# The first batch of a four-batch transformer layer reordered: queries and keys ahead of values, weight splits moved, the Hadamard fold of a weight rebuilt, one wait shortened

## The reference

```
x = x + layernorm(attention(layernorm(x)))      16 heads of 16, causal, rope on q and k
x = x + layernorm(ffn(layernorm(x)))
attention: qkv = x @ w_qkv.T + b_qkv; softmax(q k^T / 4, masked) v; @ w_out.T + b_out
ffn:       hidden = silu(x @ W1.T) * (x @ W3.T)   (1024 wide)
           hidden = fwht(hidden) / 32             (Walsh-Hadamard over the 1024)
           out = hidden @ W2.T
```

## Time and profile before

| what | value |
| --- | --- |
| three runs, us | 500.68, 498.67, 501.37 (median 500.68) |
| profiled execution: device time / span | 497.78 us / 496.1 us |
| PE busy | 405.0 us, 82% |
| DVE busy | 281.2 us, 57% |
| ACT busy | 210.9 us, 43% |
| POOL busy | 162.1 us, 33% |
| mean granted clock of PE | 0.938 |
| chain that ended last | PE 58%, DVE 13%, DMA 9%, issue 7%, ACT 6%, SP queue 3% |
| first matmul of the first attention | at 80.36 us |

### The profile page before, as it was taken

The page is one execution under the profiler, slowest core; times in us unless marked ns, Lnnn a source line. Parts: engine busy times, 40 slices in busy tenths (PEclk is TensorE's granted clock), DMA queues, the critical chain, the costliest instruction groups (busy, mean ns, idle before and its releaser), DMA issues.

```text
span 496.1 us, 7892 instructions
## 1 busy us (share of the span) xinstructions
PE 405.0 (82%) x2884; PEld 338.2 (68%) x2884; DVE 281.2 (57%) x936; ACT 210.9 (43%) x314; POOL 162.1 (33%) x284
## 2 busy tenths in 40 slices
PE   1679677999599997988599988987799979858992
PEld 1569645558489985557499975566699965448991
DVE  7554583625937776536856776267576754273114
ACT  4445234753323337843423347813332367423221
POOL 4136002533512226514422235614132245321232
PEclk9999865999969999999889999999799999997998
DMA  6549900000397000200695001102880002000001
GB/s 230 215 136 247 212 1 1 2 2 0 127 255 171 1 1 1 85 1 1 179 245 130 1 1 42 44 1 72 219 201 21 1 1 85 1 1 1 1 1 42
DMA packets 35463, 36.95 MB, mean 74 GB/s; under 512 B 2016, under 2 KB 34528, under 8 KB 35424
## 3 DMA queue, kind: packets, MB, share of 16 engines
q1 hardware_dynamic: 35424, 36.45, 26.6%
HBM read 21.76 MB, written 14.68 MB: 73 GB/s over the span
## 4 chain that ended last, share of the span: by engine, by line
PE 58%; DVE 13%; DMA 9%; issue 7%; ACT 6%; SPq 3%; POOL 2%; DVEq 0%; POOLq 0%; ACTq 0%
PE ps L266 30%; PE ps L448 8%; PE ps L464 7%; PE ps L436 5%; DMA qk_scratch<-qk_s 4%; DMA q_t<-qk_scratch 4%; ACT probs L656 4%; DVE masked_scores L923 2%; SPq L293 2%; DMA raw_bias<-in_b_out 2%; PE ps L498 2%; DVE xy L985 1%; POOL hid_s L803 1%; PE ps L405 1%; DVE stats_h L870 1%
## 5 line engine op out<-in xcount | busy, mean ns | idle before, releaser
L923 DVE CUSTOM_DVE_ANT_0 masked_scores<-ps,mask_row 128x128 bf16<-128x128 f32 (+3 forms) x256 | 114.4, 488 | 61.6 <-PE ps L436 61.1
L266 PE MATMUL ps<-xt,w_s 128*128 128x256 f32 x768 | 111.7, 294 | 0.0
L266 PEld LDWEIGHTS ps<-xt,w_s 128*128 128x128 f32 x768 | 106.2, 202 | 0.5
L803 POOL TENSOR_TENSOR hid_s<-gate,hid_s 128x512 fp32r<-128x512 f32 x32 | 41.2, 1287 | 135.9 <-ACT hid_s L668 135.9
L656 ACT ACTIVATE probs<-ps 128x1280 f32<-128x1280 f32 x64 | 76.4, 1242 | 9.5 <-PE ps L448 8.9
L436 PE MATMUL ps<-k_t,q_t 96*128 96x128 f32 (+3 forms) x256 | 71.7, 356 | 9.8 <-DMA q_t<-qk_scratch 5.6
L448 PEld LDWEIGHTS ps<-q_t,k_t 128*128 128x128 f32 x256 | 44.9, 198 | 32.2 <-ACT probs L656 14.7
L266 PE MATMUL ps<-w_s,hid_s 128*128 128x256 f32 x384 | 55.5, 284 | 7.0 <-POOL hid_s L803 7.0
L448 PE MATMUL ps<-q_t,k_t 128*128 128x512 f32 (+3 forms) x256 | 55.7, 345 | 5.6 <-ACT probs L656 4.0
L266 PEld LDWEIGHTS ps<-w_s,hid_s 128*128 128x128 f32 x384 | 51.6, 190 | 9.3 <-POOL hid_s L803 8.7
L436 PEld LDWEIGHTS ps<-k_t,q_t 96*128 96x128 f32 x256 | 43.0, 198 | 18.6 <-DVE maxima L923 10.9
(11 more groups left out here) (99 smaller groups left out, 485.3 us busy)
## 6 DMA issues: line engine op xcount, KB each, us to landing
qk_scratch<-qk_s SPq DMA_DIRECT2D x32, 256.0 KB, 5.6
k_t<-qk_scratch SPq DMA_DIRECT2D x16, 384.0 KB, 5.5
q_t<-qk_scratch SPq DMA_DIRECT2D x8, 768.0 KB, 8.8
qk_scratch<-qk_s SPq DMA_DIRECT2D x8, 512.0 KB, 5.5
xa<-in_x SPq DMA_DIRECT2D x4, 512.0 KB, 9.6
xy<-in_x SPq DMA_DIRECT2D x4, 512.0 KB, 3.5
out<-xy SPq DMA_DIRECT2D x8, 256.0 KB, 2.3
o_t<-in_w SPq DMA_DIRECT2D x1, 1024.0 KB, 10.0
```

What stands on the lines that cost most here:

```text
L266: ins = eng.matmul(o, lhs(i), rhs(j), start=first and n == 0, stop=last and n == 2, skip_group_check=skip)
L803: pool.tensor_tensor(hid_s[:, a % 2, 1, :], gate[:, a % 2, :], hid_s[:, a % 2, 0, :].bitcast(F32), ALU.subtract).then_inc(S["hid_l"], 1)
L923: ins = dve.tensor_tensor_reduce(masked_scores[:, SCORE_NO[n] % 2, i * keys:(i + 1) * keys], ps[:, banks[n], i * keys:(i + 1) * keys], mas ...
```

## The change

Six things, all but the last two in the stretch ahead of the first attention:

1. First batch: PE makes the queries and keys of tiles 0, 1, 2, 3 first and the values after (new steps `b`), each tile waiting only for its own x; 14 matmuls on zeroed keys, whose result is never read, stand at the very start of PE. `rot_s` gets a second buffer.
2. `w_qkv` is split in two halves, one on DVE, one on POOL; the bias is split in two parts, that of the output projection later; the 1/64 matrix is a POOL memset in place of an ACT copy; the x load is issued ahead of the selector.
3. The low halves of the other weights move: `wo` from POOL to DVE after the mix; `w1` and `w3` (before on DVE and POOL ahead of the units) to DVE inside the first attention, `w1` after the norm of the next x and `w3` behind the late score units. The statistics of the next x stand ahead of those units.
4. The 8-wide part of the fold of W2 is done by POOL in three butterfly stages of two additions each (L895, L896 of the new kernel), the 128-wide part by 16 matmuls on PE (`transform`, one call, behind unit 33); ACT writes the result as raw words, then the high part, DVE the low part.
5. In the first batch SP waits for the three loads of the first half before it sends the second half.
6. In every batch the first values product waits for the fifth late score unit only, not for the sixth.

The order tables of the later batches are written per engine now; in them no instruction changes its place. In the first batch the lists read as follows.

The diff, cut to its core:

```diff
-MIX = """o0 o1 d0 d1 n0 n1 q0 l0 l1 e0 c0 ...
-FIRST_MIX = "e0 c0 q0 e1 c1 q1 r0 q2 t0 r1 e2 c2 q3 t1 e3 c3 r2 t2 r3 t3".split()
+FIRST_MIX = {
+    "PE": """q0 q1 q2 r0 q3 r1 b0 b1 r2 b2 b3 r3""".split(),
+    "ACT": """q0 q1 q2 r0 q3 r1 b0 b1 r2 b2 b3 r3""".split(),
+    "DVE": """c0 r0 c1 t0 r1 c2 c3 t1 r2 t2 r3 t3""".split(),
+    "POOL": """e0 e1 e2 e3""".split(),
...
-FIRST_SELECTOR = [None, 0, 2, 9]
-FIRST_TRANSFORM = [-1, -1, -1, -1, -1, 4, 8, 13]
-FIRST_W2_PARTS = [14, 19]
+FIRST_SELECTOR = {2: 0, 3: 2}
+BUTTERFLIES_BEFORE = [0, 4, 13]
+FIRST_W2_PARTS = {"split": 18, "transform": 33, "words": 36, "high": 38}
...
                     fetch_q(0)
+                    if b == 0:
+                        sp.wait_ge(S["qk_in"], 48)
                     send(1)
...
-            sp.wait_ge(S["split_l"], 4)
+            sp.wait_ge(S["w3_l"], 1)
             load_xr(0)
...
             def qkv(b, t):
+                pe.wait_ge(S["xt_l"], b * TILES + t + 1)
...
             def values(b, g, kt):
                 if kt == 0:
                     if g == 0:
-                        pe.wait_ge(S["maxed"], (b + 1) * N_SCORES)
+                        pe.wait_ge(S["maxed"], (b + 1) * N_SCORES - 1)
...
-            def transform(c):
-                for i in range(HCH):
-                    sign = bin(i & c).count("1") % 2
-                    for s in range(2):
-                        ins = pe.matmul(ps[:, c // 2, (c % 2) * DIM:(c % 2) * DIM + DIM], had_s[:, sign, :],
-                                        w2_s[:, s, i, :], ...
+            def transform():
+                pe.wait_ge(S["had_made"], 1)
+                pe.wait_ge(S["w2_l"], 2)
+                for c in range(HCH):
+                    for part in range(2):
+                        ins = pe.matmul(ps[:, c // 2, (c % 2) * DIM:(c % 2) * DIM + DIM], had_s[:, :],
+                                        w2_s[:, part, c, :], ...
...
+            pe.wait_ge(S["zeroed"], 2)
+            for n in range(14):
+                pe.matmul(bank(7), k_t[0:QK_ROWS, 0, 0:P], k_t[0:QK_ROWS, 1, :], start=True, stop=True, ...
             pe.wait_ge(S["eye_in"], 16)
             for t in range(TILES):
                 turn_x(0, t)
-            pe.wait_ge(S["split_l"], 1)
-            pe.wait_ge(S["bias_h"], 2)
-            pe.wait_ge(S["bias_l"], 1)
-            mix(-1, FIRST_MIX)
+            pe.wait_ge(S["wqkv_l"], 2)
+            mix(-1, FIRST_MIX["PE"])
...
             for n in range(N_UNITS):
                 score_unit(0, n, FIRST_UNIT_BANKS)
+                if n == FIRST_W2_PARTS["transform"]:
+                    pe.wait_ge(S["v_copied"], TILES)
+                    transform()
...
# ACT
+                if n == FIRST_W2_PARTS["split"]:
+                    act.wait_ge(S["w2_turned"], 3)
+                    act.activation(w2_s[:, 0, :, :]..., mixed_w2, ACT.Copy).then_inc(S["w2_h"], 1)
+                if n == FIRST_W2_PARTS["words"]:
+                    act.wait_ge(S["transformed"], 1)
+                    act.activation(raw_w2, ps[:, 0:4, :]..., ACT.Copy, scale=W2_SCALE)\
+                       .then_inc(S["transformed_words"], 1)
+                if n == FIRST_W2_PARTS["high"]:
+                    act.wait_ge(S["transformed_words"], 1)
+                    act.activation(w2_s[:, 0, :, :]..., raw_w2, ACT.Copy)\
                        .then_inc(S["transformed_h"], 1)
...
# POOL
-                if t >= 1:
-                    pool.wait_ge(S["rotated"], b * TILES + t)
-                o = rot_s.rearrange("p (h e i) -> p h e i", e=2, i=HALF)
+                if t >= 2:
+                    pool.wait_ge(S["rotated"], b * TILES + t - 1)
+                o = (rot_s, rot_s_odd)[t % 2].rearrange("p (h e i) -> p h e i", e=2, i=HALF)
...
+            def butterflies(n):
+                src, dst = (raw_w2, mixed_w2) if n % 2 == 0 else (mixed_w2, raw_w2)
...
+                a, o = (w.rearrange("p (u e n) -> p u e n", e=2, n=DIM << n) for w in (src, dst))
+                pool.tensor_tensor(o[:, :, 0, :], a[:, :, 0, :], a[:, :, 1, :], ALU.add)
+                pool.tensor_tensor(o[:, :, 1, :], a[:, :, 0, :], a[:, :, 1, :], ALU.subtract).then_inc(S["w2_turned"], 1)
...
+            pool.wait_ge(S["split_h"], 1)
+            pool.tensor_tensor(wqkv_s[:, 1, 1, :], raw_wqkv[:, 3 * DIM:6 * DIM], wqkv_s[:, 0, 1, :].bitcast(F32), ALU.subtract)\
+                .then_inc(S["wqkv_l"], 1)
...
             for n in range(N_UNITS):
+                if n in BUTTERFLIES_BEFORE:
+                    butterflies(BUTTERFLIES_BEFORE.index(n))
                 max_low(0, n)
+                if n in (FIRST_W2_PARTS["split"], FIRST_W2_PARTS["split"] + 2):
+                    w2_low((n - FIRST_W2_PARTS["split"]) // 2)
...
# DVE
             def iteration(b, order, steps):
+                if order is MIX:
+                    layer_x(b + 1)
                 if b == 0:
+                    split(w2_s, raw_w2, "transformed_h", 1, "transformed_l")
                     for n in TAIL_UNITS:
                         score_unit(b, n, FIRST_UNIT_BANKS)
-                if order is MIX:
-                    layer_x(b + 1)
+                    split(w3_s, raw_w3, "split_h", 4, "w3_l")
+                    dve.wait_ge(S["transformed_l"], 1)
                 copy_o(b, 0)
                 if order is MIX:
                     norm_x(b + 1)
+                if b == 0:
+                    split(w1_s, raw_w1, "split_h", 3, "w1_l")
                 copy_o(b, 1)
```

More of the change, by code:

```diff
@@ L89, in unit_banks @@
     return banks[:-1] + [5] + TAIL_BANKS
-MIX = """o0 o1 d0 d1 n0 n1 q0 l0 l1 e0 c0 o2 d2 y0 o3 s0 n2 y1 l2 d3 s1 n3 y2 v0 l3 q1 r0 y3 s2 s3 e1 c1 t0
-    v1 e2 c2 q2 R0 r1 R1 w0 R2 R3 t1 q3 w1 r2 e3 c3 N0 N1 N2 t2 r3 N3 t3 H0 L0 H1 L1 H2 L2 H3 L3 u0 u1
-    u2 u3""".split()
-FIRST_MIX = "e0 c0 q0 e1 c1 q1 r0 q2 t0 r1 e2 c2 q3 t1 e3 c3 r2 t2 r3 t3".split()
-MIX_LAST = """o0 o1 d0 d1 n0 n1 l0 l1 o2 d2 y0 s0 n2 o3 y1 l2 d3 s1 n3 y2 v0 l3 y3 s2 s3 v1 R0 R1 w0 R2 R3 w1 N0
-    N1 N2 N3 H0 L0 H1 L1 H2 L2 H3 L3 u0 u1 u2 u3""".split()
+MIX = {
+    "PE": """o0 o1 n0 n1 q0 b0 o2 y0 o3 n2 y1 n3 y2 q1 b1 r0 y3 q2 b2 r1 q3 b3 r2 r3 H0 H1 H2 H3 u0 u1
+        u2 u3""".split(),
+    "ACT": """n0 n1 q0 b0 n2 n3 q1 b1 r0 q2 b2 r1 q3 b3 r2 S r3 H0 H1 H2 H3 u3""".split(),
+    "DVE": """o0 o1 d0 d1 l0 l1 c0 o2 d2 o3 s0 l2 d3 s1 v0 l3 r0 s2 s3 c1 t0 v1 c2 R0 r1 R1 w0 R2 R3 t1
+        w1 r2 c3 N0 N1 N2 t2 r3 N3 t3 L0 L1 L2 L3""".split(),
+    "POOL": """e0 v0 e1 v1 e2 w0 w1 e3""".split(),
+}
+FIRST_MIX = {
[3 more added lines that the diff above has]
+    "POOL": """e0 e1 e2 e3""".split(),
+}
+MIX_LAST = {
+    "PE": """o0 o1 n0 n1 o2 y0 n2 o3 y1 n3 y2 y3 H0 H1 H2 H3 u0 u1 u2 u3""".split(),
+    "ACT": """n0 n1 n2 n3 S H0 H1 H2 H3 u3""".split(),
+    "DVE": """o0 o1 d0 d1 l0 l1 o2 d2 s0 o3 l2 d3 s1 v0 l3 s2 s3 v1 R0 R1 w0 R2 R3 w1 N0 N1 N2 N3 L0 L1
+        L2 L3""".split(),
+    "POOL": """v0 v1 w0 w1""".split(),
+}
 def feed_forward_steps(units_after):
@@ L380, in qkv, with values_product @@
             def qkv(b, t):
+                pe.wait_ge(S["xt_l"], b * TILES + t + 1)
+                if t >= 2:
+                    pe.wait_ge(S["qk_copied"], b * TILES + t - 1)
+                lhs = lambda c: (lambda s: xt[:, s, c, t * P:t * P + P])
+                for c in range(CH):
+                    triple(pe, ps[:, t % 2, :], lhs(c), lambda s: wqkv_s[:, s, c, 0:2 * DIM], c == 0, False)
+                if b == 0 and t == 0:
+                    pe.wait_ge(S["sixty_made"], 1)
+                    pe.wait_ge(S["bias_s"], 1)
+                    pe.wait_ge(S["bias_l"], 1)
+                pe.matmul(ps[:, t % 2, :], sixty_fourth[:, :], bias_s[:, 0:2 * DIM], start=False, stop=True)\
+                  .then_inc(S["qk_done"], 1)
+            def values_product(b, t):
+                lhs = lambda c: (lambda s: xt[:, s, c, t * P:t * P + P])
                 if t == 0:
@@ L384, in qkv @@
                 else:
[L385 to L392, removed]
                     pe.wait_ge(S["v_copied"], b * TILES + t)
@@ L762, in iteration @@
                         xt_high(b + 1, t)
-                mix(b, order)
+                mix(b, order["ACT"])
                 feed_forward(b, steps)
@@ L832, in iteration @@
                         root(b + 1, "x")
-                for m in order:
+                for m in order["POOL"]:
                     if m[0] == "e":
@@ L909, in rotate @@
                 dve.wait_ge(S["roped_c"], b * TILES + t + 1)
-                dve.tensor_tensor(rot[:, t % 2, :], rot[:, t % 2, :], rot_s, ALU.add).then_inc(S["rotated"], 1)
+                dve.tensor_tensor(rot[:, t % 2, :], rot[:, t % 2, :], (rot_s, rot_s_odd)[t % 2], ALU.add).then_inc(S["rotated"], 1)
             def score_unit(b, n, banks):
```

147 lines of the change are left out of this document (77 added, 70 removed).

## The result

| | us |
| --- | --- |
| before, median of 6 (in the same rounds) | 500.0 (498.67 to 501.37) |
| after, median of 6 | 495.7 (494.51 to 496.56) |
| ratio, 95% interval | 0.9915 [0.9895, 0.9935] |
| profiled execution: device time / span | 495.88 / 494.2 (before 497.78 / 496.1) |
| mean granted clock of PE | 0.898 (before 0.938) |

A forecast was written before the change was run, and what follows sets the result against it. SP's queue was taken as the bound from 29.5 to 59.2 us. Gains of 5.7 up to the first attention and 1.8 from the values wait, 7.5 off 500.68, gave 493.2 us (490.7 to 495.3; wide range 489.0 to 497.8).

The forecast's parts named there:

- The start, up to T: First batch from kernel start to queries and keys of tile 0; forecast to gain 3.7 us.
- T: Time when queries and keys of tile 0 are done: 19.75 us before, forecast 16.0 (15.2 to 17.5).
- from T to the send: Rope work on tiles 0 and 1 before the first send: 8.4 us, send at 24.4, gain so far 5.1.
- SP's queue: First send to late half landed, sends and fetches now serial: 31.4 us against 29.66 before, landing at 55.8.
- From the late half to S: Late maxima, W2's fold and ACT's copies before the first attention: 18.9 us after landing, gain so far 5.7.
- S: Time of the first attention matmul: 80.36 us before, forecast 74.7.
- X: Time when DVE has done 16 heads' maxima after the late half landed, put at L + 8.1.
- L: Time when the late half has landed: 59.19 us before, forecast 55.8 (53.5 to 58.5).
- What lies beside other work: Butterfly stages, low halves of w3 and w1, next x's statistics and residual load, said to be hidden: cost nothing.
- The values wait: PE's wait for late maxima in each attention, one unit shorter: gain 1.8 us over four batches (0.5 to 2.4).
- the slower one: Rival: DVE's maxima hold POOL's port, so POOL makes W2's fold late; 504.5 us, chance 0.04.
- starts little: Rival: slow leading matmuls and the DVE/POOL lock leave little gain at the start; 495.3 to 498.1 us, chance 0.22.

The follow-up runs named there:

- rot_all: Changed kernel with the old wait on the single rope buffer in all four batches; 492.11 us.
- no_gate: Changed kernel without SP's wait for the first fetch ahead of the second send; 492.02 us.
- w2_early: Changed kernel with ACT's high half of the turned W2 two units earlier, at unit 16 instead of 18; 494.54 us.
- w3_late: Changed kernel with DVE's low halves of w3 and w1 put behind its copies of the first and second output; 493.24 us.
- rot_single: Changed kernel with the old wait on the single rope buffer in batches 1 to 3, two buffers in the first only; 492.50 us.
- changed_again: The changed kernel itself, unedited, timed and profiled a second time; 494.77 us.
- no_warm: Changed kernel without the 14 leading matmuls on zeroed keys; 495.24 us.

## Why the prediction was right, and where its sizes were off

*The start, up to T, and from T to the send*: right, 16.13 for 16.0 and 24.44 for 24.4, but by luck: two errors stood against each other. "The norm of x still starts at 10.29 ... so putting x first in the queue gains nothing" was false: it started at 9.41, because POOL's second root step took 0.20 us in place of 1.08 once DVE's 1536-element subtraction no longer ran beside it, and it then took 1.5 us more beside POOL's half of wqkv. rot_all shows that the send, forecast between T + 7.1 and T + 9.0, came at T + 8.3 only because of the second rope buffer; it would have been T + 7.5. The lock was worth 0.8 there, not the 1.9 between the two ends.

*SP's queue*: the term "this edit alone costs 1.7 to 1.9" was mis-sized; no_gate measures about 3.0. The forecast took the second send at the 6.0 us of the first; it took 7.4 (6.7 to 7.6 in the eight traces with the gate). The other side of the comparison, 29.66 us of before, was right: 29.5 in no_gate. Why the second send takes longer than the first isn't shown.

*From the late half to S*: 19.9 for 18.9. The fold started at X + 1.3, not X + 0.4: ACT's copy behind the turn ended at L + 4.8, not L + 3.6, and POOL at L + 9.6. w2_early removes the late start, 0.6 of it. ACT's two copies end 0.6 after DVE's last maximum, as said (0.7).

*What lies beside other work*: "All nothing" failed. I asked whether w3's low half delays DVE's own next copy, and not what else it stops: POOL's 0.2 us step stood for it, and PE behind that. 1.3 us, by w3_late. The rule that I had quoted for the start applied here.

*The second `rot_s` in later batches*, "0 to 0.2, nothing": about 0.5 a batch by rot_single, 1.4 in all.

*The values wait*: right, 1.8 with the split that was given (0.6, 0.3, 0.3, 0.6); only batch 0's part lay behind the lock.

The mis-sized terms, 2.2 to S (74.7 against 76.94), 1.3 and 1.4, sum to 4.9, and 5.6 are missing in the pair of traces (7.5 less 1.9). With changed_again the terms are 1.4 to S, 1.3 and 1.4, in sum 4.1, and 3.8 are missing (span 492.4). The medians miss 3.2, so part of the agreement is scatter. Up to S the stretches ran as forecast (the queue, then maxima, the fold and ACT's two copies) and only their sizes were off; behind S "all nothing" was wrong. The wide range held, and the 490.7 to 495.3 of the forecast itself did not. Of the rivals, the slower one didn't occur: POOL's 1024-element steps took 2.34 us each beside DVE's maxima, so those don't hold the port. The rival "starts little" had the right time (495.3 to 498.1) for the wrong reason: the start gained what was forecast.

## What to carry to other kernels

A wait that an engine no longer has is work that starts earlier somewhere else: ask whom it then runs beside. Here POOL's freed rope products and DVE's "hidden" weight subtraction each held up a short step on the other engine, and PE stood behind it; before an instruction of 2 us goes into a gap, list what the other engine has to do in those 2 us. A transfer order should be tried without its gate before it is kept, and single gains of less than 1% should be added by their landmarks in the traces, not by their medians.

## What the runs showed of the hardware

- DVE and POOL hold each other up in both directions. POOL's 128x6 subtraction took 1.94 us beside DVE's 2048-element one and 0.20 without. DVE's add took 1.01 or 1.20 us beside POOL's rope products and 0.69 without, and its norm of x, which reads one tile, 2.89 us for 1.38 beside POOL's 1.96 us step. The Trainium skill ("SBUF — State Buffer", "SBUF: two separate sides") says that whichever starts first holds the pair for the whole instruction; all of these rows agree. One pair of before doesn't: POOL's root step on 4 elements had run since 8.09 us, for 1.01 us, when DVE's subtraction of 1536 elements began at 8.43, and it took 1.76 us, what its 2.29 us for 2048 elements give (an estimate: 1.72). And beside DVE's maxima, with their scores in PSUM, POOL took 4.68 us for two steps of 1024 elements, 2.3 ns an element as alone.
- Fourteen matmuls of 512 columns ahead of the first transposes made six later ones take 1.61 us in place of 2.90, 2.2 us after the last of the 14 had ended and with the transposes between (no_warm). The profile's granted clock is 1.00 from 12 to 16 us in both kernels, so here only the durations tell the two rates apart.
- The stretch from S to the first values product took 11.55 us in one execution of the changed kernel and 10.72 in another. In the first, the matmul sets at 82.43 and 84.62 took 1.43 and 1.27 us; in the other the set at 81.60 took 1.38 and the next, at 83.33, 0.74. The rate rose one head earlier; the granted clock of the stretch is 0.60 and 0.69.
